# Cross-attention heads: five maximum tiles of a head issued in the head ahead of it, one of them between the outputs and the rows of maxima

## The reference

```python
q = _qdq(x) @ _qdq(wq).T + bq            # x normalized; 256 x 512
kv = cond @ wkv.T + bkv                  # context of 4096 rows
k, v = jnp.split(kv, 2, axis=-1)         # 16 heads of 32 columns each
attn = jax.nn.softmax(jnp.einsum('bnhd,bmhd->bhnm', q, k) * scale, axis=-1)
o = jnp.einsum('bhnm,bmhd->bnhd', attn, v).reshape(B, N, C)
out = _qdq(o) @ _qdq(wp).T + bp
```

## Time and profile before

| what | value |
|---|---|
| median of 3 runs | 602.35 us (602.3 to 602.77) |
| the profiled execution's own time | 602.53 us |
| its span, first to last instruction | 600.5 us |
| TensorE busy / VectorE busy / ScalarE busy / GpSimd busy | 98% / 64% / 50% / 44% of the span |
| granted TensorE clock | 1.000 of full speed |
| matmuls of maximum tiles at L1440 | 240 |

### The profile page before, as it was taken

One profiled execution on the slowest core, in us unless ns is written; L12 is line 12 of the kernel. 1 busy time (PEld: TensorE's weight loads), 2 busy tenths in 40 slices (PEclk: granted clock), 3 DMA queues, 4 the chain that ended last, 5 costly groups with the idle time before them and its releaser, 6 DMA issues.

```text
span 600.5 us, 12582 instructions
## 1 busy us (share of the span) xinstructions
PE 585.7 (98%) x4269; PEld 469.8 (78%) x4270; DVE 384.6 (64%) x688; ACT 301.7 (50%) x439; POOL 266.9 (44%) x142
## 2 busy tenths in 40 slices
PE   8999999999999999999999999999999999999997
PEld 7888888888887667666776676766898889799996
DVE  4999430340434888888888888897664235475562
ACT  3544233233233566556666655565368677645441
POOL 0000933113124888788888888870103644400000
PEclk9999999999999999999999999999999999999999
DMA  8865734524638654545554555500142224245410
GB/s 289 328 229 189 221 126 168 198 95 166 191 125 270 201 166 153 180 156 169 160 153 153 158 169 161 155 38 1 35 176 72 86 106 160 83 199 211 159 50 36
DMA packets 34223, 92.20 MB, mean 154 GB/s; under 512 B 6928, under 2 KB 11024, under 8 KB 30480
## 3 DMA queue, kind: packets, MB, share of 16 engines
q1 hardware_dynamic: 32944, 89.68, 45.2%
q10 hardware_dynamic: 1248, 2.10, 0.9%
HBM read 65.02 MB, written 18.35 MB: 139 GB/s over the span
## 4 chain that ended last, share of the span: by engine, by line
PE 86%; ACT 4%; DVE 4%; issue 2%; POOL 2%; DMA 1%; ACTq 0%; POOLq 0%; SPq 0%; DVEq 0%
PE ps L348 16%; PE ps L349 15%; PE ps L350 15%; PE ps L1578 10%; PE ps L1566 10%; PE ps L1440 9%; PE ps L1592 3%; ACT p_ring L785 3%; POOL l_ring L680 2%; PE ps L1544 1%; DVE m_part L1067 1%; PE ps L1649 1%; DMA f_ring<-stream 1%; PE ps L1458 1%; PE ps L1532 1%
## 5 line engine op out<-in xcount | busy, mean ns | idle before, releaser
L1067 DVE TENSOR_REDUCE m_part<-ps 128x1 f32<-128x512 f32 x240 | 150.8, 683 | 20.5 <-PE ps L1440 20.2
L785 ACT ACTIVATE p_ring<-ps 128x1024 f32<-128x1024 f32 x128 | 124.5, 1022 | 69.2 <-PE ps L1578 28.7
L634 POOL TENSOR_TENSOR p_sum<-p_sum,p_ring 128x1024 f32<-128x1024 f32 x42 | 100.1, 2383 | 3.7
L1566 PEld LDWEIGHTS ps<-q_stack,k_stack 98*128 98x128 f32 x512 | 75.0, 189 | 16.3 <-ACT p_ring L785 6.6
L1566 PE MATMUL ps<-q_stack,k_stack 98*128 98x256 f32 x512 | 85.2, 289 | 1.3
L1440 PE MATMUL ps<-k_stack,q_max 96*128 96x512 f32 x240 | 85.5, 417 | 0.1
L609 POOL TENSOR_TENSOR v_all<-v_all,bv_row 128x512 f32 (+1 forms) x32 | 41.7, 1320 | 74.8 <-ACT v_all L747 74.3
L1578 PE MATMUL ps<-p_ring,v_head 128*32 128x256 f32 x960 | 64.6, 383 | 0.0
L1026 DVE SCALAR_TENSOR_TENSOR kl_buf<-ps,biases,kh_buf 128x512 fp32r<-128x512 f32 x32 | 23.7, 749 | 56.0 <-ACT kh_buf L735 55.6
L348 PE MATMUL ps<-xt_h,h_ring 128*128 128x256 f32 x200 | 57.0, 285 | 1.8 <-POOL l_ring L680 1.8
L321 DVE TENSOR_TENSOR l_ring<-f_ring,h_ring 128x2048 fp32r<-128x2048 f32 x22 | 50.2, 2288 | 12.5 <-ACT h_ring L317 12.5
(11 more groups left out here) (225 smaller groups left out, 1168.1 us busy)
## 6 DMA issues: line engine op xcount, KB each, us to landing
f_ring<-stream SPq DMA_DIRECT2D x29, 1024.0 KB, 4.9
k_stack<-kh_scratch SPq DMA_DIRECT2D x128, 128.0 KB, 2.6
kh_scratch<-kh_buf SPq DMA_DIRECT2D x32, 256.0 KB, 5.7
kl_scratch<-kl_buf SPq DMA_DIRECT2D x32, 256.0 KB, 6.1
k_stack<-kl_scratch SPq DMA_DIRECT2D x64, 128.0 KB, 2.6
v_head<-v_all SPq DMA_DIRECT2D x16, 512.0 KB, 2.9
v_all<-stream SPq DMA_DIRECT2D x4, 256.0 KB, 4.7
f_ring<-stream SPq DMA_DIRECT2D x4, 256.0 KB, 5.8
```

The costliest lines, as they stand in the source:

```text
L634: nc.gpsimd.tensor_tensor(p_sum[:, p, :], p_ring[:, 0, :] if n == 0 else p_sum[:, p, :], p_pair[:] if c == 3 else p_ring[:, c % 4, :], ALU ...
L785: nc.scalar.activation(p_ring[:, c % 4, :], ps[:, 2 * (c % 2):2 * (c % 2) + 2, :].rearrange("p b n -> p (b n)"), ACT.Exp, scale=XSCALE).th ...
L1067: nc.vector.reduce_max(m_part[:, j // NT, j % NT:j % NT + 1], maximum_bank(j), AX.X).then_inc(max_read, 1)
L1566: last = nc.tensor.matmul(ps[:, 2 * (c % 2) + k // 2, (k % 2) * N:(k % 2 + 1) * N], k_stack[p][0:SPLIT_ROWS + MAX_ROWS, at128(4 * c + k)], ...
```

## The change

On TensorE, tile 4 of head h + 2 moves out of head h + 1 (where it stood behind score chunk 0) into head h, at its end behind tile 3. Tile 2 moves from behind `value(7)` to a place between `value(6)` and `maximum_rows`. Within the head, the tiles are divided anew among the places between the score chunks, so that each place up to chunk 3 holds as many as before (the tile numbers are one higher), the place behind the denominators holds one instead of two, the one behind chunk 4 two instead of one, and the one behind chunk 5 one instead of two. VectorE's stream takes the tiles in the same order as before; only the bounds of the calls move.

```diff
-            chunk_maxima(1, 0, 4)
+            chunk_maxima(1, 0, 5)
...
-                chunk_maxima(h + 1, 4, 12)
+                chunk_maxima(h + 1, 5, 12)
...
-                    chunk_maxima(h + 2, 1, 4)
+                    chunk_maxima(h + 2, 1, 5)
...
+                def maxima_after(start, end):
+                    if after_loads is not None:
+                        maxima(h + 2, p, after_loads, start, end)
+
                 score(0)
-                next_maxima(4, 5)
+                next_maxima(5, 6)
                 score(1)
-                next_maxima(5, 7)
+                next_maxima(6, 8)
                 score(2)
-                next_maxima(7, 9)
+                next_maxima(8, 10)
                 score(3)
-                next_maxima(9, 10)
+                next_maxima(10, 11)
                 if not first:
                     summed_denominators(h - 1, 1 - p)
-                next_maxima(10, 12)
+                next_maxima(11, 12)
                 score(4)
-                next_maxima(12, 13)
+                next_maxima(12, 14)
                 score(5)
-                next_maxima(13, 15)
+                next_maxima(14, 15)
                 for c in range(4):
                     value(c)
                 next_maxima(15, 16)
-                if after_loads is not None:
-                    maxima(h + 2, p, after_loads, 0, 1)
+                maxima_after(0, 1)
                 score(6)
                 if not first:
                     merge(h - 1)
                 score(7)
-                if after_loads is not None:
-                    maxima(h + 2, p, after_loads, 1, 2)
+                maxima_after(1, 2)
                 for c in range(4, 7):
                     value(c)
+                maxima_after(2, 3)
                 maximum_rows(h + 1)
                 value(7)
-                if after_loads is not None:
-                    maxima(h + 2, p, after_loads, 2, 4)
+                maxima_after(3, 5)
...
-            maxima(1, 1, 1, 2, 4)
+            maxima(1, 1, 1, 2, 5)
```

## The result

The changed kernel takes 607.38 us (607.28 to 607.55), against 602.38 us of the kernel before in the same runs: a ratio of 1.0082, 95% interval 1.0067 to 1.0097. It is slower by 5.0 us. Its profiled execution took 607.28 us, with a span of 605.3.

A forecast was written before the change was run, and what follows sets the result against it. TensorE, busy for 98% of the span, was taken as the bound. Round trips of 4.6 us and waits of 0.65 made 5.2 us, on 602.35 giving 607.5, rounded to 607.4 us; range 603.0 to 609.9.

The forecast's parts named there:

- The bound and the mechanism: TensorE bounds the kernel; full-width tile 2 between output chunk 6 and the rows of maxima makes a fourth round trip.
- The size of the round trip: At tile 2 among the outputs: 0.14 us leaving full width, 0.19 coming back, 0.33 in 14 heads, 4.6 us.
- the upper bound I gave for the rows: At the rows of maxima behind tile 2: round trip plus 0.11 us for unfetched weights, 0.44, 6.2 us in all.
- The wait for the normalization: Tile 2 waits for `o_done` of the head before: 0.05 us in 13 heads, 0.65 us.
- my sign of "some 0.42": In the profile after, a chain piece of some 0.42 us for tile 2 between output chunk 6 and the rows.
- Tile 4 ahead of score chunk 0: "nothing": Tile 4's waits for `mrow_ready` and its keys cost nothing; ScalarE's wait at score chunk 2 stays.
- tile 2's earlier reduction: In VectorE's stream: its idle time ahead of tile 2 is cut in two, and nothing is gained.
- Ahead of head 0 and at the end: Tile 4 joins tiles 2 and 3 before the first score chunk 0: +0.24 us, given back in head 14.
- The sum: Over the whole kernel: 4.6 us of round trips and 0.65 of waits, 5.2 us slower.
- the waits put down to VectorE at tiles 10 and 15 are real: Faster rival: at tiles 10 and 15, 2 x 0.19 us a head go; -3.4 us in all, 599.0; chance 0.10.
- The normalization as a bound: Slower rival: late normalization holds tile 2 by 0.65 us in 13 heads; 13.1 us with trips, 615; chance 0.04.

The follow-up runs named there:

- the run behind the rows: The changed kernel with tile 2 one step later, between the rows of maxima and output chunk 7: 607.35 us.

## Why the prediction was right, point by point

- **The bound and the mechanism.** TensorE's own stream is the bound, and a full-width tile among the quarter-width outputs costs a switch there and back. Four runs bear it out from different sides: one trip more costs 0.316 us a head, one less gives 0.297, tile 2 alone with its wait costs 0.329, and a tile of a quarter's width in the same stretch, with no wait, costs nothing. The merge shows that it isn't the number format.
- **The size of the round trip.** Forecast 0.33, measured 0.28 in the changed kernel: the stretch grew by 0.57, of which 0.24 is the tile and 0.05 the wait. Coming back cost the 0.19 of the earlier trace rows. Leaving cost 0.09 and not 0.14, because the rows of maxima follow and not an output chunk; with a chunk behind it (the run behind the rows) it is 0.14. So the upper bound I gave for the rows, another 0.11, was on the wrong side.
- **The wait for the normalization.** Forecast 0.05, measured 0.46 - 0.41 = 0.05. It is the part that the switch doesn't hide; moved one output chunk ahead it grows to 0.48 (0.89 - 0.41), and with no switch over it some 0.2 show. Two small slips: the rows give 0.05 from an end to the load it releases, not the 0.06 that I used (the changed kernel has 319.98 - 319.93 = 0.05 too), and my sign of "some 0.42" for tile 2's piece of the chain, measured 0.48, left this wait out.
- **Tile 4 ahead of score chunk 0: "nothing".** This holds in the changed kernel, but by luck: the reason I gave was incomplete. I looked at its own waits and not at what its early place does to the tiles behind it. Alone it costs 3.6 us in bank waits; it is free only beside an early tile 2. By the same omission I took tile 2's earlier reduction to be worth nothing: it is worth nothing against the kernel before, and 0.24 us a head (14.370 - 14.127) once tile 4 is early.
- **Ahead of head 0 and at the end.** Forecast +0.24 and -0.24; measured +0.64 with head 0's round trip (0.57 forecast for the two) and -0.25. What the other 0.07 is stays open.
- **The sum.** 5.2 forecast, 5.0 measured. In the 13 heads between the marks it is 0.38 forecast and 0.319 measured; part of the nearness of the total is luck, the 0.21 us of scatter ahead of the heads, which no term of mine held. In the 13 heads the trip came out 0.05 smaller than forecast, the wait as forecast.
- **The rivals.** That the waits put down to VectorE at tiles 10 and 15 are real has fallen: the gap ahead of the tile behind the denominators and ahead of tile 15 is still 0.41, though the reduction that tile 11 waits for, the sixth of nine that take 5.59 us from 307.91, ends near 311.7, and its weights are loaded at 312.27; and full-width denominators take the first of the two gaps away. The normalization as a bound is right as a mechanism, one output chunk further up (613.47 us), and the margin to it is as thin as forecast.

The Trainium skill's TensorEngine Tiling (Array Packing), section Key Properties, says that a change of tiling mode drains the engine, and the runs agree: the load of the new width begins only 0.07 us before the old stream ends (312.27 against 312.34, 417.29 against 417.36), and it is the width that costs. The Trainium skill's TensorE: Matmul & The Clock Gate, section Single matmul latency, gives for a single bf16 matmul 166 ns beyond its streaming; the measured 0.28 to 0.33 us a round trip are nearly twice that, and the measurement decides.

## What to carry to other kernels

On an engine that is the bound, count how often its stream changes between matmuls of full width and of a quarter's width: here each round trip costs about 0.3 us, whatever other engine the gap's label names. So place a matmul beside others of its width, or give it that width, before looking for a place that serves the other engines. And where tiles share a ring of banks, one tile moved ahead alone can bring later tiles to their banks before these are free, as tiles 5, 7 and 9 here: try the parts of such a change alone, since they don't add.

## What the runs showed of the hardware that was not expected

- A wait can hide under a switch of width: the same normalization holds a full-width tile 2 by 0.05 us beyond the switch, and a quarter-width one by some 0.2 (0.41 for the tile against 0.22 without the wait).
- Leaving full width costs 0.14 us ahead of an output chunk and 0.09 ahead of the two-column rows of maxima.
- Four full-width F32R matmuls of 256 columns take 0.47 us where eight narrow ones took 0.57 and 0.19 more behind them, 0.29 us dearer.
- The idle time on the weight loads' row is no measure of a switch's price: the return to full width costs 0.19 us with a gap of 0.41 (behind outputs) and with one of 0.22 (behind the rows of maxima).
